# Masked scores in one pass over a bank pair with wrapped keys, and the high/low splits moved off VectorE

## What is computed

```
for i in range(6):                                    # DEPTH
    x = attn_layer(shift_tokens(x), Wqkv[i], ...) + x
    x = ffn_layer(shift_tokens(x), ...) + x

shift_tokens: the second half of the channels is moved one token later
attn_layer:   qkv = x @ Wqkv (16 heads of 64); q, k normalised and rotated;
              windows of 32 queries attend to their own and the previous window:
              sim = q k^T * 8, masked where key > query or key < query - 32
              out = softmax(sim) @ v;  return out @ Wo
ffn_layer:    layernorm, x @ W1 (2 x 341), a * gelu(gate), @ W2
```

## Time and profile before

| | |
|---|---|
| median of 3 runs | 4308.0 us (4307.14 to 4308.48) |
| the profiled execution, own time | 4310.28 us |
| its span, first to last instruction | 4308.2 us |
| PE (TensorE) / DVE (VectorE) busy | 3648.7 us (85%) / 3618.5 us (84%) |
| ACT (ScalarE) / POOL (GpSimd) busy | 3063.5 us (71%) / 2732.3 us (63%) |
| mean granted TensorE clock | 0.956 of full speed |

### The profile page before, as it was taken

How to read it: one execution, slowest core, us unless ns; L and a number is a source line. 1 busy time by engine, 2 the same in 40 slices (tenths; PEclk the granted TensorE clock), 3 DMA queues, 4 the chain that set the end, 5 groups by cost and what they waited for, 6 DMA issues and landing times. The chain is left out here.

```text
span 4308.2 us, 109724 instructions
## 1 busy us (share of the span) xinstructions
PE 3648.7 (85%) x31072; PEld 2319.1 (54%) x31072; DVE 3618.5 (84%) x12131; ACT 3063.5 (71%) x8807; POOL 2732.3 (63%) x4419
## 2 busy tenths in 40 slices
PE   5887688898888888888988888888888888898884
PEld 2444355555555555555555555555555555555552
DVE  7999688889888888888888888888887888888873
ACT  3443477777777777777787777777776777877774
POOL 0000577777777777677776776777776767777771
PEclk8999799999999999999999999999999999999997
DMA  1000322222222222222222222222222222222221
GB/s 45 6 7 12 106 92 90 85 90 96 90 88 90 82 95 93 87 93 84 84 101 91 93 87 80 88 95 88 99 84 79 94 95 89 94 85 89 86 78 61
DMA packets 225228, 352.55 MB, mean 82 GB/s; under 512 B 41535, under 2 KB 68349, under 8 KB 224381
## 3 DMA queue, kind: packets, MB, share of 16 engines
q1 hardware_dynamic: 224604, 345.22, 23.4%
HBM read 125.41 MB, written 5.77 MB: 30 GB/s over the span
## 5 line engine op out<-in xcount | busy, mean ns | idle before, releaser
L964 POOL TENSOR_SCALAR pr<-pr,rden 128x128 f32<-128x128 f32 (+1 forms) x3072 | 1134.4, 388 | 931.7 <-DVE rden L1219 930.6
L852 ACT ACTIVATE pr<-sm,nb,rq 128x128 f32<-128x128 f32 (+1 forms) x3072 | 1515.9, 498 | 44.7 <-DVE nb L1246 39.4
L971 POOL TENSOR_TENSOR rot<-ab,swp 128x512 f32<-128x512 f32 x768 | 984.4, 1282 | 509.7 <-DMA swp<-ab 508.5
L1194 DVE TENSOR_TENSOR ab<-bank,ltab 128x512 f32<-128x512 f32 x1536 | 985.4, 683 | 281.3 <-PE bank L292 260.8
L1240 DVE CUSTOM_DVE_ANT_0 sm<-bank,mask 128x128 f32<-128x128 f32 (+1 forms) x3072 | 841.3, 330 | 55.9 <-issue 52.2
L840 ACT ACTIVATE sq<-bank 128x512 f32<-128x512 f32 x768 | 451.6, 588 | 256.7 <-DVE ab L1194 255.0
L852 ACT ACTIVATION_READ_ACCUMULATOR pr<-sm,nb,rq 128x1 f32 x3072 | 587.8, 191 | 0.0
L634 PE MATMUL bank<-ident,pr 128*128 128x128 f32 x1536 | 407.1, 291 | 210.1 <-DVE pt L1226 208.3
L1226 DVE COPY pt<-bank 128x512 f32<-128x512 f32 x768 | 531.5, 692 | 10.2
L625 PEld LDWEIGHTS bank<-rot 64*64 64x64 f32 x12288 | 291.9, 133 | 452.8 <-issue 452.4
L977 POOL TENSOR_TENSOR rot<-rot,rkb 128x512 f32<-128x512 f32 x384 | 497.7, 1296 | 44.2 <-DMA rkb<-k_scratch 44.2
(11 more groups left out here) (156 smaller groups left out, 6503.7 us busy)
## 6 DMA issues: line engine op xcount, KB each, us to landing
swp<-ab SPq DMA_DIRECT2D x1536, 128.0 KB, 2.0
rkb<-k_scratch SPq DMA_DIRECT2D x768, 128.0 KB, 2.9
raw<-Wqkv SPq DMA_DIRECT2D x48, 128.0 KB, 2.2
gg<-xT SPq DMA_DIRECT2D x48, 128.0 KB, 2.3
gg<-xT SPq DMA_DIRECT2D x48, 127.5 KB, 2.4
raw<-Wqkv SPq DMA_DIRECT2D x12, 256.0 KB, 2.7
wo<-Wo SPq DMA_DIRECT2D x6, 512.0 KB, 4.2
k_scratch<-rsum SPq DMA_DIRECT2D x192, 8.0 KB
```

What stands on the lines that cost most here:

```text
L852: ins = act.activation(pr[:, s % 4, i, cs], sm[:, s % 2, i, cs], ACT.Exp, bias=nb[:, s, t, i:i + 1], scale=head_scale(rq, p, b)[:, t, i:i ...
L964: ins = pool.tensor_scalar(pr[:, e % 4, i, cs], pr[:, e % 4, i, cs], rden[:, e, t, i:i + 1], 1.0, ALU.mult, ALU.mult)
L971: pool.tensor_tensor(rot[:, PAIRS * (j % 2) + j // 2, :], ab[:, j % 2, 0, :], swp[:, j % 2, :], ALU.add).then_inc(qk_rot, 1)
L1194: ins = dve.tensor_tensor(seqs(ab[:, j % 2, i, :]), seqs(use_bank("qk", j)[:, :]), ltab[:, 2 * (j % 2) + i:2 * (j % 2) + i + 1, :] .to_bro ...
```

## The change

It has four parts.

1. **Scores.** The second half gets 128 columns instead of 160: the 32 earlier keys, which only queries 128 to 159 use, are wrapped into columns 96 to 127 of the half, where for the first 64 query rows nothing allowed stands. `SCORE_TILES` has five entries instead of four (96, 96, 64, 32 and 96 columns), so a step has ten products instead of eight. Banks 0 and 1 become one tensor `pair`.
2. **Maxima and probabilities.** `maxima` is one addition of the mask over both banks (128 x 512, into `sm`), a wait on its semaphore, and one maximum reduction of `sm` (128 x 512 to 4 values, into `mx` in PSUM). The exponentials are all 128 wide. `normalise` is one GpSimd product of 128 x 512 with a broadcast second operand. `copy_probs` gets, behind its copy and a wait for it, a clearing of 32 x 64 elements of `pt`; `p_Tsb` is raised only after it.
3. **x.** At step 8 SyncE copies the next x, shifted, to a new buffer `xs2` with two DMAs (behind the swap of the step; it waits for the previous split). At step 11 ScalarE makes the high part (after `square`), at step 14 GpSimd the low part, each as one 128 x 512 instruction.
4. **Weights.** `split_low` moves from VectorE to GpSimd, behind `rotate` and ahead of `scale_k`, one step later or in the same step as before (`SPLIT_AT` plus one; in T2 at steps 1 and 2), and so do the eight splits ahead of the first turn.

```diff
-SCORE_TILES = [(0, 0, 0), (1, 32, 32), (2, P, P - WINDOW), (3, P + 64, P + 32)]
+SCORE_TILES = [(0, 0, 0, 96), (1, 32, 32, 96), (2, P, P, 64), (2, 2 * P - WINDOW, P - WINDOW, WINDOW), (3, P + WINDOW, P + WINDOW, 96)]
...
+        pair = ctx.enter_context(nc.psum_tensor("pair", [P, 2, GT], F32))
+        bank = [pair[:, 0, :], pair[:, 1, :]]
...
+                def shift_next(x):
+                    done = held(sp_e, n.n[1] + 2) if cur is not None else None
+                    src = seqs(xT[:, bass.ds(x * GT, GT)])
+                    if done is not None:
+                        sp_e.wait_ge(x_split, done)
+                    sp_e.dma_start(seqs(xs2[:, :])[0:64], src[0:64]).then_inc(xs2_in, 16)
+                    sp_e.dma_start(seqs(xs2[:, :])[64:128, :, 1:SEQ], src[64:128, :, 0:SEQ - 1]).then_inc(xs2_in, 16)
...
+                    if s == 8 and gs[2] is not None:
+                        shift_next(gs[2])
...
-                    for half, c, k0 in SCORE_TILES:
+                    for half, c, k0, kn in SCORE_TILES:
...
-                            mm = pe.matmul(bank[i][part, c:c + 96], rot[rows, p, c0 + 64 * half:c0 + 64 * half + 64],
-                                           rot[rows, PAIRS + p, c0 + k0:c0 + k0 + 96], start=True, stop=True)
+                            mm = pe.matmul(bank[i][part, c:c + kn], rot[rows, p, c0 + 64 * half:c0 + 64 * half + 64],
+                                           rot[rows, PAIRS + p, c0 + k0:c0 + k0 + kn], start=True, stop=True)
...
-                            cs = slice(0, P) if t == 0 else slice(P, UW)
+                            cs = slice(t * P, t * P + P)
                             ins = act.activation(pr[:, s % 4, i, cs], sm[:, s % 2, i, cs], ACT.Exp,
...
+                def split_high_x(buf):
+                    landed = held(act, n.z[32] + 64 if cur is not None else n.z[32] + 32)
+                    settle(act)
+                    act.wait_ge(xs2_in, landed)
+                    act.activation(xh[:, buf, :, :], seqs(xs2[:, :]), ACT.Copy).then_inc(x_hi, 1)
...
+                    if s == 11 and gs[2] is not None:
+                        split_high_x(par)
...
+            def split_low(layer, c):
...
+                pool.wait_ge(w_hi, made)
+                src, hi, lo = chunk_views(c)
+                pool.tensor_tensor(lo, src, hi.bitcast(F32), ALU.subtract).then_inc(w_lo, 1)
...
-                    for i in range(2):
-                        for t in range(2):
-                            cs = slice(0, P) if t == 0 else slice(P, UW)
-                            ins = pool.tensor_scalar(pr[:, e % 4, i, cs], pr[:, e % 4, i, cs],
-                                                     rden[:, e, t, i:i + 1], 1.0, ALU.mult, ALU.mult)
+                    dst = pr[:, e % 4, :, 0:2 * P].rearrange("p i (t c) -> p i t c", t=2)
+                    ins = pool.tensor_tensor(dst, dst, rden[:, e, :, :].rearrange("p t i -> p i t").unsqueeze(3)
+                                             .to_broadcast([P, 2, 2, P]), ALU.mult)
...
+                    pool.wait_ge(x_hi, made)
+                    pool.tensor_tensor(xl[:, buf, :, :], seqs(xs2[:, :]), xh[:, buf, :, :].bitcast(F32), ALU.subtract)\
+                        .then_inc(x_split, 1)
...
+                    if s - 1 in SPLIT_AT.get(kind, ()):
+                        split_low(nl, SPLIT_AT[kind][s - 1])
+                    if kind == "T2" and s in (1, 2):
+                        split_low(nl, 5 + s)
...
+                    if s == 14 and gs[2] is not None:
+                        split_low_x(par)
...
-                    dve.transpose(pt[96:128, e % 4, :, 0, P:P + WINDOW], pr[0:32, e % 4, :, P:P + WINDOW])
-                    dve.tensor_copy(pt[:, e % 4, :, :, 0:P],
-                                    bank[2][:, :].rearrange("p (i t c) -> p i t c", i=2, t=2)).then_inc(p_Tsb, 1)
+                    dve.transpose(pt[96:128, e % 4, :, 2 * P:UW], pr[0:32, e % 4, :, 2 * P - WINDOW:2 * P])
+                    dve.tensor_copy(pt[:, e % 4, :, 0:2 * P],
+                                    bank[2][:, :].rearrange("p (i c) -> p i c", i=2)).then_inc(p_copy, 1)
+                    dve.wait_ge(p_copy, n16 + (16 * q + e + 1))
+                    dve.memset(pt[96:128, e % 4, :, 0:WINDOW], 0.0).then_inc(p_Tsb, 1)
...
-                    for i in range(2):
-                        for t in range(2):
-                            cs = slice(0, P) if t == 0 else slice(P, UW)
-                            ins = dve.tensor_tensor_reduce(sm[:, s % 2, i, cs], bank[i][:, cs], mask[:, cs],
-                                                           1.0, -3e38, ALU.add, ALU.max, mx[:, t, i:i + 1])
-                    ins.then_inc(sc_max, 1)
+                    dst = sm[:, s % 2, :, 0:2 * P]
+                    dve.tensor_tensor(dst, pair[:, :, 0:2 * P], mask[:, :].unsqueeze(1).to_broadcast([P, 2, 2 * P]),
+                                      ALU.add).then_inc(sc_mask, 1)
+                    dve.wait_ge(sc_mask, n16 + (s + 1))
+                    dve.tensor_reduce(mx, dst.rearrange("p i (t c) -> p i t c", t=2), AX_X, ALU.max)\
+                        .then_inc(sc_max, 1)
...
-                    if gs[2] is not None and s == 11:
-                        if cur is not None:
-                            dve.wait_ge(v_proj, n8 + 8)
-                        split_high_x(gs[2], par)
-                    if gs[2] is not None and s in (13, 14):
-                        split_low_x(gs[2], par, n1 + 3 if cur is not None else n1 + 2, s - 13)
...
+    wrapped = np.where((q < 64) & (own >= P - WINDOW), own - P, own)
...
-    mask = np.concatenate([band(own), band(wide)], 1)
+    mask = np.concatenate([band(own), band(wrapped)], 1)
```

More of the change, by code:

```diff
@@ L117, in build @@
         sm = sb("sm", [P, 2, 2, UW])
-        pr = sb("pr", [P, 4, 2, UW])
-        pt = sb("pt", [P, 4, 2, 2, P + WINDOW])
+        pr = sb("pr", [P, 4, 2, 2 * P])
+        pt = sb("pt", [P, 4, 2, UW])
+        xs2 = sb("xs2", [P, GT])
         rkb = sb("rkb", [P, KSLOT, GT])
@@ L127, in build @@
         ltab = sb("ltab", [P, 4, SEQ])
-        mask = sb("mask", [P, UW])
+        mask = sb("mask", [P, 2 * P])
         ident = sb("ident", [P, P])
@@ L145, in build @@
         eps = sb("eps", [P, 1])
-        bank = [ctx.enter_context(nc.psum_tensor(f"bank{i}", [P, GT], F32)) for i in range(8)]
+        pair = ctx.enter_context(nc.psum_tensor("pair", [P, 2, GT], F32))
+        bank = [pair[:, 0, :], pair[:, 1, :]]
+        bank += [ctx.enter_context(nc.psum_tensor(f"bank{i}", [P, GT], F32)) for i in range(2, 8)]
         k_dram = nc.dram_tensor("k_scratch", (2, 2, 4, GT), F32, kind="Internal").ap()
@@ L152, in build @@
         vt_f = vtok[:, :, :].rearrange("p a n -> p (a n)")
-        mx = bank[1][:, UW:UW + 4].rearrange("p (t i) -> p t i", t=2)
+        mx = pair[:, 1, 2 * P:2 * P + 4].rearrange("p (i t) -> p i t", i=2)
         xtok = rotw[:, 0:TOKENS].rearrange("p (t c) -> p t c", c=DIM)
@@ L211, in build @@
         k_norm = sem("k_norm")
-        sc_ps, sc_max, sc_bias, p_exp, p_rden, p_norm, p_T, p_Tsb, o_ps, o_sb = (
-            sem(n) for n in ("sc_ps", "sc_max", "sc_bias", "p_exp", "p_rden", "p_norm", "p_T", "p_Tsb", "o_ps", "o_sb"))
+        sc_ps, sc_mask, sc_max, sc_bias, p_exp, p_rden, p_norm, p_T, p_copy, p_Tsb, o_ps, o_sb = (
+            sem(n) for n in ("sc_ps", "sc_mask", "sc_max", "p_copy", "sc_bias", "p_exp", "p_rden", "p_norm", "p_T", "p_Tsb", "o_ps", "o_sb"))
         at_out, at_add = sem("at_out"), sem("at_add")
-        xs_in = sem("xs_in")
+        xs_in, xs2_in = sem("xs_in"), sem("xs2_in")
         f_cen, f_xc, f_sq, f_var, f_ln, f_rstd, f_xn, f_gb, f_hi, f_split = (
@@ L633, in transpose_probs @@
                     for i in range(2):
-                        pe.transpose(bank[2][:, 256 * i:256 * i + P], pr[:, e % 4, i, 0:P], ident[:, :])
+                        pe.transpose(bank[2][:, 256 * i:256 * i + P], pr[:, e % 4, i, P:2 * P], ident[:, :])
                         mm = pe.transpose(bank[2][:, 256 * i + P:256 * i + 2 * P],
-                                          pr[:, e % 4, i, P + WINDOW:UW], ident[:, :])
+                                          pr[:, e % 4, i, 0:P], ident[:, :])
                     mm.then_inc(p_T, 1)
@@ L653, in outputs @@
                                 mm = pe.matmul(bank[3][64 * i:64 * i + 64, cols], vtok[:, 2 * b + t, ch],
-                                               pt[:, e % 4, i, t, 0:cols.stop - cols.start],
+                                               pt[:, e % 4, i, P - P * t:P - P * t + cols.stop - cols.start],
                                                start=(b == 0 and t == 0), stop=True, skip_group_check=True)
@@ L937, in _ @@
                 split_high(0, c)
-            flow(act, turn, (1, 2, 3, 4, 8, 16))
+            flow(act, turn, (1, 2, 3, 4, 8, 16), (32,))
             with act.Fori(0, GROUPS) as g:
@@ L949, in _ @@
```

(30 more changed lines are left out.)

7 lines of the change are left out of this document (2 added, 5 removed).

## The result

The changed kernel takes 4326.17 us (median of 5 runs, 4324.78 to 4334.66) against 4308.37 us: a ratio of 1.0043, 95% interval [1.0028, 1.0058]. It is slower, as forecast, but by 18 us where 47 were worked out, and that small number is the difference of large ones. It lies inside the 4320 to 4395 us that the prediction gave its own case.

What follows compares the result with a forecast made beforehand. Bounds: TensorE in steps 0 to 9, VectorE in 9 to 12, ScalarE ending last around 13 and 14. 1.25 us per turn made 60 us, less 16, plus 3: 47 us, so 4355 us predicted, range 4250 to 4445 us.

Steps and rivals of the forecast that it cites:

- its own case: The whole kernel at 4355 us, with 4320 to 4395 us for the unknown sizes; chance 0.50.
- Maxima and clearing: VectorE, every step: maxima 0.25 us longer, clearing 0.26 us more, counted only in stretches where they lie on the path.
- VectorE time in steps 9 to 12, and little of either at 13 and 14: Pricing rule: VectorE time counts in steps 9 to 12, TensorE time in 0 to 9, little of either at 13, 14.
- Casts: VectorE, step 11: removing the casts of x saves 1.42 us per turn, in the stretch where VectorE is the bound.
- Low halves: VectorE, steps 13 and 14: removing 2.29 and 0.71 us gives nothing, since gelu and its table loads are waited for.
- Weights: Low parts off VectorE save 16 us in all inside turns; the first eight on GpSimd cost about 3 us.
- Scores: TensorE: two more products cost 0.10 us per step, counted where TensorE is the bound.
- GpSimd, ScalarE, the DMAs: Moved x and weight work, broadcast product and new x copies cost nothing, covered by idle time or early issue.
- the signs named: Start to bias 1.45 us, copy to next 0.86, scores 0.59, VectorE above 84%, transposes' wait above 3, longer squares wait.
- slower yet: VectorE becomes the bound in all steps and its whole load counts, 2.9 us per turn: 4450 us; chance 0.13.
- faster: Removing the step 12 cast lump outweighs additions near their lower bounds, -1.0 us per turn: 4250 us; chance 0.27.
- no change: Scores cost nothing, the rest as in the sum, +9 us; range 4300 to 4316 us; chance 0.10.

Runs made afterwards that it cites:

- attn_only: Kernel before with parts 1 and 2 of the change only, x and weights split on VectorE as before: 4507.93 us, 1.0460.
- scores_only: Kernel before with its third score tile cut into 64 and 32 columns, ten products instead of eight: 4309.29 us, 0.9987.
- experiment 5: Changed kernel with x splits back on VectorE, casts at step 14, low halves at 15: 4378.14 us; with casts at 11, low halves at 13 and 14: 4460.56 us.
- low_back: Changed kernel with the low half of x back on VectorE at steps 13 and 14, from the new buffer: 4321.72 us, 1.0025.
- weights_only: Kernel before with only the weights' low parts moved to GpSimd: 4276.41 us, 0.9918.
- four_norm: Changed kernel with GpSimd's four 128-wide normalise products in place of the one broadcast product: 4332.38 us, 1.0053.

## Why the prediction was wrong

The sign and the durations held; the weights of nearly all terms were off. The additions and both removals were all priced too low.

**Maxima and clearing** (sum: 0.3 + 1.42 + 0.15 = 1.87 us per turn, 90 us; the 0.3 holds 0.1 for the scores and is itself rounded up from 0.23). Measured in the changed kernel, 97 us for the clearing and 115 for the maxima, the latter against four 128-wide instructions, 0.32 us per step. Both at once give 158 us from there, and all of parts 1 and 2 cost 198 us on the kernel before, with nothing for the scores. The failed step is "VectorE time in steps 9 to 12, and little of either at 13 and 14", priced one for one as three maxima, two clearings and 0.15 us, with no term for TensorE's clock. The path that it followed, from the copy to TensorE, was the right one. The table gives the length of a turn in three stretches, from the bias of one step to that of another (us, means over 45 of the 48 turns of one trace each, the first and the last two left out):

| | step 0 to 9 | 9 to 13 | 13 to next 0 | turn |
|---|---|---|---|---|
| before | 42.47 | 18.03 | 18.04 | 78.54 |
| `attn_only` | 42.89 | 20.78 | 18.99 | 82.66 |
| measured difference | 0.42 | 2.75 | 0.95 | 4.12 |
| in the sum, scores included | 1.0 | 1.42 | 0.25 | 2.67 |

The sum's stretches match these roughly. From 9 to 13 every one of four steps is longer, by 0.64, 0.57, 0.70 and 0.84 us, where about 0.5 was forecast for three of them. From 13 on the delay is not hidden either: TensorE's wait for ScalarE's squares grows from 98 to 153 us, mostly between the biases of steps 14 and 15. And of the 198 us, TensorE is busy for 117 and idle for 81; the scores alone account for 29 of the busy time (`scores_only`), the other 88, an estimate from these pages, go with a clock of 0.938 in place of 0.956, a cost that the sum had at nothing. Clock and delay were not varied one without the other. The transposes' own waits do not carry the difference; in `attn_only` they come to 204 us, against 210 before, and as above all of them are for the clearing, whatever name the row has:

```profile
PE bank L636 <- POOL pr L964: 201.8, 142, 3.0
...
PE bank L636 <- DVE pt L1229: 2.3, 4, 0.7
```

The other terms:

- **Casts** (sum: 1.42 us, 68 us): 134 us. The place was right and the size was not, for the reasons of experiment 5: stretched beside GpSimd, ahead of the copy, and paid again in TensorE's clock after the stall.
- **Low halves** (sum: nothing): right, as far as `low_back` shows it.
- **Weights** (sum: -16 and +3): -35 on the kernel before, -46 behind the additions. In the trace of `weights_only` the load turn and T0, with three splits each, are together 4.5 us shorter per layer, 23 us in all, where 16 were forecast; the turns with one split each, named as hidden, give 6 us in all, between -1.3 and 2.7 each. The rest lies in turns that hold no split and is not explained.
- **Scores** (sum: 0.10 in eight steps, 38 us): nothing. The size was 0.05, and the step that failed is the addition along the path: steps 0 to 4 and the stretch to the centring product were both charged, though a delay of TensorE ahead of a wait for someone else is eaten by that wait.
- **GpSimd, ScalarE, the DMAs** (nothing): right for GpSimd, with `four_norm`; the broadcast product was even shorter than the 1.3 us assumed. ScalarE's copy and the DMAs were not tested by themselves.
- **The first turns**: not in the sum beyond 3 us; they lose ten, almost all of it by the additions.

Of the signs named, these came: 1.44 and 0.90 us, VectorE's share at 84.3%, the longer wait for the squares. These did not: the transposes wait 2.7 us per turn and not above 3, the scores take 0.54 and not 0.59, and VectorE is busy 27 us longer in all and not 2.9 us per turn, 139 us.

In the sum's terms the forecast was 128 - 68 - 13, and the runs gave 198 - 134 - 46. The errors are 70, 66 and 33 us, and they cancel down to 29: that the time came out as near as it did is luck. The rival "slower yet" overcharged the additions (8.2 us per turn, 394 us) by more than the sum undercharged them. The rival "faster" was nearer for the removals, and had the reason, "the lump of casts ahead of the copy", but put the additions lower still. The "no change" rival's own sum, 4317 us, lies just outside the range that it was given.

## What to carry to other kernels

When a change adds work in every step and takes away a lump in one, price both in every step that has no slack, and add what the clock of the waiting engine costs: here that was some 88 of the 198 us between the kernel before and `attn_only`. Where a wait has two conditions, the name in the row is only the one that landed last; count which instance was waited for before you draw a chain from it. Fewer instructions are not always faster: two that pass all elements twice took 1.44 us, four fused ones with their accumulator reads 1.12. A small clearing with its own wait (0.30 us) could here be folded into the copy out of PSUM. And charge a delay only up to the next wait for someone else.

## What was not expected of the hardware

GpSimd's 128 x 512 product in which the second operand is one value per 128 columns takes 1042 ns, that with two full operands 1281 to 1287 ns. A product of PSUM with an SBUF table takes VectorE 692 ns, exactly as a plain copy out of PSUM. A cast of 64 x 512 takes 0.42 us beside an idle GpSimd and 1.45 us beside a GpSimd subtraction that started 0.1 us before it; the profile books the difference as VectorE's busy time, not as idle time.
